# Moving v, the second layer norm and two steps of the max pass to other groups of the loop

## The chip, the cores and the metric

The kernel runs on one core of a Trainium2 chip. The metric is the device time of one execution in microseconds (us). The inputs are 16 sequences of 512 tokens with 128 features, in float32.

## The reference

Per sequence, one transformer layer, with the layer norm behind each residual sum:

```python
qkv = x @ c_attn_w + c_attn_b                      # 128 -> 3 * 128, 16 heads of 8
scores = q k^T / sqrt(8), causal;  attn = softmax(scores)
# heads 0, 1, 2: attn * mult (1.6 in a third of the keys), then normalised again
x = layernorm(x + (attn @ v) @ c_proj_w + c_proj_b)
h = [x, -x];  h = s0 * (h @ W0);  h = relu(h) * 2   # 256 -> 512, weights +-1
h = s1 * (h @ W1);  h = relu(h) * 2                 # 512 -> 512
x = layernorm(x + s2 * (h @ W2))                    # 512 -> 128
```

## The kernel before

**Iterations, groups, steps.** The program is a software pipeline written out by hand. An iteration `n` has four groups of ten steps, and (g, t) below is step t of group g, counted from 0; the words "first group" to "fourth group" are g = 0 to 3. In each step TensorE (PE) does one or two steps of the max pass (`max_scores`, line 946), one step of the scores (`scores`, line 970), in every second step a quarter of the sums of attention times v (`sums`, line 1005), and then what `PLACES` puts there. Work of four sequences runs at once: iteration n does the scores, exponentials and sums of sequence n, the max pass of n and n + 1, q and k of n + 2, v of n + 1, the projection and first layer norm of n - 1 and most of the feed-forward layers of n - 1 and n - 2.

**The max pass.** Before a score is exponentiated the row's maximum is known: PE computes the scores once for `max_ps`, a ring of three PSUM banks, and VectorE (DVE) takes the maximum of each row (`take_max`, line 774). There are 40 such steps in an iteration. `MAX_TWICE` lists the steps with two, `MAX_NONE` those with none; before, the four groups have 13, 10, 7 and 10. The first ten belong to sequence n's last quarter. After the tenth, POOL (GpSimd) splits the maxima into three bf16 parts (`split_rowmax`, lines 529 to 535), PE transposes them ("rowmax1", line 1015, step (1, 0)), DVE copies them out (`take_rowmaxT`, line 796) and ScalarE (ACT) issues a DMA that puts them beside q in `stack` (`rowmax_rows`, line 662). The scores of step (2, 0) wait for that DMA (`rowmax_in[1]`). The same happens with "rowmax0" in (3, 3) and (3, 4) for the next sequence's first half; the scores of (0, 0) of the next iteration wait for it (`rowmax_in[0]`).

**PSUM banks of the fillers.** All work of `PLACES` shares the two banks of `bank_ps` in turn. A row of the table is (what, which sequence, PE's step, the step in which DVE or ACT empties the bank). PE's `claim` waits until the use before the last one has been emptied. ACT empties the feed-forward outputs with two activations, `h_hi` (line 654) and `full` (line 633), behind the exponential of that step.

**v.** Eight fp32 matmul passes on PE (line 1069) and four instructions of DVE (`take_v`, lines 807, 812, 814) in steps (0, 7) and (0, 8), for sequence n + 1. The sums of the next iteration are the first to need it.

**Second layer norm.** `layernorm_stats` and `layernorm_var` (DVE, lines 833, 839, 842, 843), then `normalise_tokens` (POOL, lines 539, 542, 549) and `store` (the DMA to the output, issued by SP). Before, DVE does it for sequence n - 2 in (2, 1) and (2, 2), POOL between two masks of the third group, and SP issues the store as the last item of its iteration. The first layer norm is in (1, 8) and (1, 9), and the transposes of its result, "x1T", in (2, 5).

**SP's queue.** In an iteration SP issues, in this order: nine DMAs that copy the second half of q and k into `stack` (`later_half`, line 379), the load of x for `x_in`, nine DMAs of the first half (`earlier_half`, after the scores of the second group), the load of `x_res` (after it has waited for `rowmax_in[0]`), and the store.

**POOL's queue.** The masks of the exponentials (line 511), the splits of q and k (lines 494, 496), of the maxima, and the low parts of the feed-forward activations (line 519) run on POOL in a fixed order. "ffn1_1", "ffn1_2" and "ffn1_3" have their low parts at the start of the iteration.

Of the kernel before, what the change touches and what calls it, by code (L numbers as in the profile page):

```python
# [49 lines left out]
    ("q", 2, (0, 3), (0, 4)),  # L50
    ("k", 2, (0, 4), (0, 5)),
    ("ffn2T", -2, (0, 5), (0, 7)),
    ("v", 1, (0, 7), (0, 8)),
    ("ffn2", -2, (0, 9), (0, 9)),
    ("rowmax1", 0, (1, 0), (1, 1)),
    ("tok_0", -1, (1, 1), (1, 1)),
# [6 lines left out]
    ("ffn0_2", -1, (3, 0), (3, 1)),  # L63
    ("ffn0_3", -1, (3, 1), (3, 3)),
    ("rowmax0", 1, (3, 3), (3, 4)),
    ("ffn1_0", -1, (3, 6), (3, 7)),
    ("ffn1_1", -1, (3, 8), (3, 9)),
)
# [27 lines left out]

NEGMAX_ROWS = ((3, 5), (1, 2))

LN_STATS = ((1, 8), (2, 1))
LN_VAR = ((1, 9), (2, 2))  # L100
LN_STATS_OF_END = ((1, 2), (3, 4))
LN_VAR_OF_END = ((1, 2), (3, 5))

MAX_TWICE = ((0, 1), (0, 3), (0, 5))
MAX_NONE = ((2, 1), (2, 2), (2, 7))

COPIES_OF_POOL = ((1, 0), (1, 1), (0, 2), (2, 0), (2, 1), (2, 2))
POOL_COPIES_FOR = ((0, 0), (0, 1))
# [27 lines left out]
def block_kernel(nc, x, w_qkv, b_qkv, w_proj, b_proj, k0, k1, k2, s0, s1, s2, out):  # L136
    B, S, D = x.shape
# [17 lines left out]
    def live(b):  # L155
        return 0 <= b.c < B

    def behind_attention(n):

        return n.c == B  # L160
# [15 lines left out]
    def use_of(b, what):  # L176

        return use(b + -BATCH_OF[what], what)

    with ExitStack() as ctx:  # L180
        def sb(name, shape, dt=F32):
            return ctx.enter_context(nc.sbuf_tensor(name, shape, dt))
# [58 lines left out]
        res2 = sb("res2", [P, T, D])  # L241
# [68 lines left out]
        def max_steps(n, g, t):  # L310

            each = [2 if (g_, t_) in MAX_TWICE else 0 if (g_, t_) in MAX_NONE else 1
                    for g_ in range(G) for t_ in range(STEPS)]
# [11 lines left out]
        def last_batch(b):  # L325

            return b.c == B - 1

        def res1_of(b):

            return x_in if last_batch(b) else res1

        def split_by_dve(b, what):

            return last_batch(b) or (behind_attention(b + 2) and what == "ffn1_3")
# [10 lines left out]
        def _(sp):  # L346
# [35 lines left out]
            def store(b):  # L382
                sp.wait_ge(ln_step[1], b.times(4, 4))
                sp.dma_start(out_tok[b.times(1)], res2[:]).then_inc(stored, 16)

            def later_half(n):
                b = n + 1
                if not live(b) or (b.c == 0):
                    return
                sp.wait_ge(split_step, b.times(3, 3))  # L390
                if b.c == 1:
                    sp.wait_ge(stacked[b.parity][0], 9 * 16)
                if live(n + -1):
                    sp.wait_ge(scored, (n + -1).times(G * STEPS, 4 * STEPS))
                stack_half(b, 1)
# [21 lines left out]
                stack_half(b, 0)  # L417

            def iteration(n):
                later_half(n)  # L420
                b = n + 3
                if live(b):
                    wait_full(sp, use_of(b + -1, "xT"))
                    sp.dma_start(x_in[:], x_tok[b.times(1)]).then_inc(x_loaded, 16)
                earlier_half(n)
                if live(n + 1):
                    sp.wait_ge(rowmax_in[0], (n + 1).times(16, 16))
                if live(n):
                    if n.c > 0:
                        wait_free(sp, use_of(n + -1, "proj"))  # L430
                    sp.dma_start(x_res[:], x_tok[n.times(1)]).then_inc(xres_loaded, 16)
                if live(n + -2):
                    store(n + -2)

            run(iteration)
            sp.wait_ge(stored, 16 * B)
# [3 lines left out]
        def _(pool):  # L440
# [112 lines left out]
            def iteration(n):  # L553
                def low(layer, m):
                    b = n + (-2 if layer and m else -1)
                    if live(b) and not split_by_dve(b, f"ffn{layer}_{m}"):
                        low_part_by_pool(b, layer, m)

                def bias_residual():
                    b = n + -1  # L560
                    if live(b):
                        pool.wait_ge(xres_loaded, b.times(16, 16))
                        nc.gpsimd.tensor_tensor(x_res[:], x_res[:], bp[:].unsqueeze(1).broadcast_to([P, T, D]),
                                                ALU.add).then_inc(xres_biased, 1)

                def split_qk(k):
                    b = n + 2
                    if live(b) and not (b.c == 0):
                        split(b, k)

                def layernorm_out(i):
                    b = n + (-2 if i else -1)
                    if live(b):
                        normalise_tokens(b, i)

                def masks(g, k):
                    if live(n):
                        mask(n, g, k)

                def rowmaxes(half):  # L580
                    b = n + (0 if half else 1)
                    if live(b):
                        split_rowmax(b, half)

                low(1, 1)
                low(1, 2)
                low(1, 3)
                masks(0, 0)
                split_qk(0)
                masks(0, 1)  # L590
                rowmaxes(1)
                masks(0, 2)
                split_qk(2)
                bias_residual()
                masks(1, 0)
                masks(1, 1)
                masks(1, 2)
                layernorm_out(0)
                masks(2, 0)
                layernorm_out(1)  # L600
                masks(2, 1)
                low(0, 0)
                masks(2, 2)
                rowmaxes(0)
                low(0, 1)
                low(0, 2)
                low(0, 3)
                masks(3, 0)
                masks(3, 1)
                low(1, 0)  # L610
                masks(3, 2)
# [110 lines left out]
        def _(dve):  # L722
# [107 lines left out]
            def layernorm_stats(b, i, src):  # L830
                wait_free(dve, use_of(b, "ffn2" if i else "proj"))
                for t in range(T):
                    ins = nc.vector.bn_stats(stats[:, t, :], src[:, t, :])
                ins.then_inc(ln_step[i], 1)
# [22 lines left out]
            def iteration(n):  # L857
                for g in range(G):
                    for t in range(STEPS):
                        for b, quarter, step in max_steps(n, g, t):  # L860
                            take_max(b, quarter, step)
                        for what, d, _, step in places(n):
                            b = n + d
# [23 lines left out]
                        for what in SPLIT_STEPS:  # L887
                            b = n + BATCH_OF[what]
# [5 lines left out]
                            elif split_by_dve(b, what):  # L894
# [2 lines left out]
                                if not last_batch(b):  # L897
                                    dve.wait_ge(split_ready, b.times(9, 8))
                                low_part(b, 1 + FT * layer + m, h_hi[layer][:, m, :], h_lo[layer][:, m, :])
                        ln_stats, ln_var = LN_STATS, LN_VAR  # L900
                        if behind_attention(n):
                            ln_stats, ln_var = LN_STATS_OF_END, LN_VAR_OF_END
                        if (g, t) == ln_stats[0] and live(n + -1):
                            layernorm_stats(n + -1, 0, res1_of(n + -1))
                        if (g, t) == ln_stats[1] and live(n + -2):
                            layernorm_stats(n + -2, 1, res2)
                        if (g, t) == ln_var[0] and live(n + -1):
                            layernorm_var(n + -1, 0)
                        if (g, t) == ln_var[1] and live(n + -2):
                            layernorm_var(n + -2, 1)  # L910

            run(iteration)

# [231 lines left out]
```

## Time and profile before

| | us |
|---|---|
| median of 3 runs | 920.17 (919.77 to 925.36) |
| the profiled execution: its time | 922.26 |
| its span in the profile | 919.5 |
| an iteration in the middle of the run | 51.6 |

The profile gives busy time per engine: PE 835.0 us (91%), DVE 621.4 (68%), ACT 608.3 (66%), POOL 527.3 (57%). PE's matmuls are pipelined and their ends are modelled, so a busy PE is not one that nothing holds up: the short waits of its weight loads (PEld) and the chain of waits tell more. TensorE's granted clock is 1.00 of full speed in the middle of the run and 0.96 on the mean of the span, so the middle iterations can be compared with each other.

### The profile page before, as it was taken

Reading aid. Unit: us, or ns where it says so; the run is one execution under the profiler, and the core shown is the slowest. Engines: PE = TensorE matmul, PEld = TensorE weight load, DVE = VectorE, ACT = ScalarE, POOL = GpSimd, SP = SyncE. Lnnn points to the kernel's source line nnn. Section 1 sums busy time; section 2 is a strip of 40 time slices with the busy share of each in tenths; the row PEclk is TensorE's granted clock in tenths of the full one; section 3 lists DMA queues with packets and bytes.
Section 4 is the critical chain, followed back from the end, with each engine's and each line's share of the span. In section 5 each row is a group of like instructions: output and inputs, shape, how many; then the busy total and the mean of one; then the engine's idle time right before and its main releaser. Section 6 shows DMA issues by size and latency. Waiting matters only on the chain.

```text
span 919.5 us, 17053 instructions
## 1 busy us (share of the span) xinstructions
PE 835.0 (91%) x5696; PEld 427.4 (46%) x5696; DVE 621.4 (68%) x2617; ACT 608.3 (66%) x1091; POOL 527.3 (57%) x763
## 2 busy tenths in 40 slices
PE   4488599999999999999999999999999999999875
PEld 1133244545455554545454554545454554545353
DVE  3487386685958587685858587685869587774124
ACT  3036267686776777676776777677776778586743
POOL 4215146575756657575756657575756658384732
PEclk9669699999999999999999999999999999999988
DMA  5735545545353545545352545545353535300000
GB/s 106 87 46 66 65 57 63 68 48 86 42 81 45 74 50 74 67 49 91 36 83 44 74 51 76 63 49 85 45 81 45 77 39 75 50 14 13 24 1 23
DMA packets 65741, 53.16 MB, mean 58 GB/s; under 512 B 5015, under 2 KB 63351, under 8 KB 65655
## 3 DMA queue, kind: packets, MB, share of 16 engines
q1 hardware_dynamic: 63542, 49.72, 39.7%
q0 software_dynamic: 960, 1.58, 1.4%
q10 hardware_dynamic: 1152, 0.79, 0.6%
q8 instruction: 45, 0.74, 0.4%
q14 instruction: 42, 0.34, 0.2%
HBM read 9.24 MB, written 4.19 MB: 15 GB/s over the span
## 4 chain that ended last, share of the span: by engine, by line
PE 60%; DVE 13%; ACT 7%; POOL 7%; issue 7%; DMA 5%; SPq 1%; POOLq 0%; DVEq 0%; ACTq 0%
PE av_ps L1005 11%; PE max_ps L946 11%; PE bank_ps L1032 9%; PE score_ps L970 8%; PE bank_ps L1033 7%; DVE max_ps L774 7%; PE bank_ps L929 4%; POOL res L549 3%; PE bank_ps L1080 3%; DMA stack<-parts 2%; ACT full L633 2%; ACT e L641 2%; DMA stack<-rowmaxT 2%; PE bank_ps L1047 2%; POOL rstd L539 2%
## 5 line engine op out<-in xcount | busy, mean ns | idle before, releaser
L774 DVE CUSTOM_DVE_ANT_0 max_ps<-max_ps,future 128x512 f32<-128x512 f32 (+3 forms) x1024 | 477.6, 517 | 233.9 <-PE max_ps L946 230.4
L641 ACT ACTIVATE e<-score_ps 128x512 f32<-128x512 f32 x640 | 371.3, 613 | 255.9 <-PE score_ps L970 254.6
L946 PE MATMUL max_ps<-stack 72*128 72x512 bf16 (+3 forms) x1024 | 247.6, 312 | 20.8 <-DMA stack<-parts 12.8
L970 PE MATMUL score_ps<-stack 75*128 75x512 bf16 (+3 forms) x1024 | 244.1, 303 | 17.6 <-DMA stack<-rowmaxT 10.6
L511 POOL TENSOR_SCALAR_AFFINE_SELECT e<-e 128x512 f32<-128x512 f32 x256 | 160.1, 637 | 172.2 <-ACT e L641 172.0
L519 POOL TENSOR_TENSOR h_lo<-full,h_hi 128x512 fp32r<-128x512 f32 x119 | 151.5, 1278 | 84.0 <-ACT full L633 83.9
L1005 PE MATMUL av_ps<-e,vaug 128*25 128x512 f32 (+3 forms) x2048 | 191.3, 447 | 0.0
L946 PEld LDWEIGHTS max_ps<-stack 72*128 72x128 bf16 x1024 | 81.3, 99 | 156.5 <-issue 94.0
L774 DVE DVE_READ_ACCUMULATOR2_ANT rowmax<- 128x1 f32 x1024 | 143.8, 140 | 0.0
L970 PEld LDWEIGHTS score_ps<-stack 75*128 75x128 bf16 x1024 | 91.2, 98 | 91.5 <-ACT e L641 35.0
L1032 PE MATMUL bank_ps<-h_hi,w 128*128 128x512 f32 x256 | 109.6, 428 | 0.4 <-DVE h_lo L854 0.4
L1033 PE MATMUL bank_ps<-h_lo,w 128*128 128x512 f32 x256 | 102.7, 401 | 0.0
L654 ACT ACTIVATE h_hi<-bank_ps,scales 128x512 fp32r<-128x512 f32 x128 | 90.8, 709 | 11.0 <-PE bank_ps L1033 10.8
L633 ACT ACTIVATE full<-bank_ps,scales 128x512 f32<-128x512 f32 x128 | 91.6, 716 | 0.0
L1005 PEld LDWEIGHTS av_ps<-e,vaug 128*25 128x25 f32 x2048 | 37.6, 102 | 69.5 <-issue 63.6
L549 POOL TENSOR_SCALAR res<-res,rstd,shift 128x128 f32<-128x128 f32 x120 | 59.5, 509 | 3.1
L1032 PEld LDWEIGHTS bank_ps<-h_hi,w 128*128 128x128 f32 x256 | 49.1, 192 | 24.8 <-ACT full L633 10.6
L539 POOL TENSOR_TENSOR rstd<-var_eps,minus_half 128x4 f32<-128x4 f32 x32 | 32.6, 1017 | 39.6 <-DVE var_eps L843 39.6
L1033 PEld LDWEIGHTS bank_ps<-h_lo,w 128*128 128x128 f32 x256 | 49.1, 192 | 9.2
L494 POOL TENSOR_TENSOR qk<-qk,parts 128x1024 f32<-128x1024 f32 x15 | 32.1, 2140 | 34.6 <-ACT qk L633 34.5
L1080 PE MATMUL bank_ps<-xT,wqk 128*128 128x512 f32 x64 | 39.1, 703 | 1.9 <-ACT xT L633 1.9
L496 POOL TENSOR_TENSOR parts<-qk,parts 128x1024 bf16<-128x1024 f32 x15 | 32.0, 2134 | 11.6 <-ACT parts L716 11.6
(95 smaller groups left out, 725.8 us busy)
## 6 DMA issues: line engine op xcount, KB each, us to landing
stack<-parts SPq DMA_DIRECT2D x276, 128.0 KB
x_in<-in_L_attn_hidden_states SPq DMA_DIRECT2D x16, 256.0 KB, 15.2
x_res<-in_L_attn_hidden_states SPq DMA_DIRECT2D x16, 256.0 KB, 2.9
out_x<-res SPq DMA_DIRECT2D x16, 256.0 KB, 3.4
stack<-parts POOLq DMA_DIRECT2D x12, 128.0 KB, 12.9
stack<-rowmaxT ACTq DMA_DIRECT2D x32, 24.0 KB
e<-in_L_ffn_k SPq DMA_DIRECT2D x1, 256.0 KB, 3.3
e<-in_L_attn_c_attn_w SPq DMA_DIRECT2D x1, 128.0 KB, 2.9
```

The lines of the kernel that those rows point to most:

```text
L511: last = nc.gpsimd.affine_select(out=ap, in_=ap, compare_op=ALU.is_ge, fill=0.0, base=0, pattern=[[0, 4], [1, P]], channel_multiplier=-1)
L519: nc.gpsimd.tensor_tensor(h_lo[layer][:, m, :], whole, hi.bitcast(F32), ALU.subtract).then_inc(split_ready, 1)
L549: ins = nc.gpsimd.tensor_scalar(x[:, t, :], x[:, t, :], rstd[:, i, t:t + 1], shift[:, i, t:t + 1], ALU.mult, ALU.add)
L633: nc.scalar.activation(out_ap, bank_ps[:, u[0], :], func, **kw).then_inc(bank_free[u[0]], 1)
L641: nc.scalar.activation(e[g % 2][:, t, :], score_ps[:, t % 2, :], ACT.Exp, scale=SCALE).then_inc(exped, 1)
L654: nc.scalar.activation(hi, bank_ps[:, u[0], :], func, **kw)
L774: return nc.vector.tensor_tensor_reduce(out=scored_block, in0=scored_block, in1=future[:, P * (T - 1 - qt):S], scale=1.0, scalar=NEG, op0= ...
L946: return nc.tensor.matmul(out_ap[:, col:col + width], st[0:QK_ROWS, h, 0, P * qt:P * qt + P], st[0:QK_ROWS, h, 1, 0:width], start=True, st ...
L970: return nc.tensor.matmul(out_ap[:, col:col + width], st[0:ALL_ROWS, h, 1, P * kt:P * kt + P], st[0:ALL_ROWS, h, 0, P * kt:S], start=True, ...
L1005: last = nc.tensor.matmul(av_ps[32 * j:32 * j + ODD, P * kt:S], vals, src, start=(order == 0 and not odd), stop=(order == 3 and odd == 1))
L1032: nc.tensor.matmul(bank, w, hi, start=(i == 0), stop=False)
L1033: last = nc.tensor.matmul(bank, w, lo, start=False, stop=(i == len(pairs) - 1))
```

## The change

`v` is dropped from (0, 7) and (0, 8) and put at (3, 4) on PE and (3, 5) on DVE, still for sequence n + 1. The max pass gets two more double steps, (0, 7) and (0, 8), and two more empty ones, (1, 1) and (1, 2), so the groups have 15, 8, 7 and 10. The second layer norm of a sequence is done one iteration later, in (0, 0) (DVE), behind the low part of ffn1_1 (POOL), and its store is now the first item of SP's iteration, ahead of `later_half`; only for the last two sequences it stays in the iteration where it was, in (3, 4) and (3, 5).

```diff
-    ("v", 1, (0, 7), (0, 8)),
...
     ("rowmax0", 1, (3, 3), (3, 4)),
+    ("v", 1, (3, 4), (3, 5)),
     ("ffn1_0", -1, (3, 6), (3, 7)),
...
-LN_STATS = ((1, 8), (2, 1))
-LN_VAR = ((1, 9), (2, 2))
-LN_STATS_OF_END = ((1, 2), (3, 4))
-LN_VAR_OF_END = ((1, 2), (3, 5))
-
-MAX_TWICE = ((0, 1), (0, 3), (0, 5))
-MAX_NONE = ((2, 1), (2, 2), (2, 7))
+LN1_STEPS = ((1, 8), (1, 9))
+LN2_STEPS = ((0, 0), (0, 0))
+LN1_STEPS_OF_END = ((1, 2), (1, 2))
+LN2_STEPS_OF_END = ((3, 4), (3, 5))
+
+MAX_TWICE = ((0, 1), (0, 3), (0, 5), (0, 7), (0, 8))
+MAX_NONE = ((1, 1), (1, 2), (2, 1), (2, 2), (2, 7))
...
+        def second_norms(n):
+
+            if live(n + -3) and n.c - 3 < B - 2:
+                yield n + -3, LN2_STEPS
+            if n.c - 2 >= B - 2:
+                yield n + -2, LN2_STEPS_OF_END
...
             def iteration(n):
+                for b, steps in second_norms(n):
+                    if steps == LN2_STEPS:
+                        store(b)
                 later_half(n)
...
-                if live(n + -2):
-                    store(n + -2)
+                for b, steps in second_norms(n):
+                    if steps == LN2_STEPS_OF_END:
+                        store(b)
...
                 low(1, 1)
+                second_layernorm_out(LN2_STEPS)
                 low(1, 2)
...
-                layernorm_out(0)
+                layernorm_out()
                 masks(2, 0)
-                layernorm_out(1)
+                second_layernorm_out(LN2_STEPS_OF_END)
                 masks(2, 1)
```

## Rows read from the trace of the kernel before

**Rows 1.** Busy time by stretch, the four groups of one iteration (columns: stretch, length, five engines, clock, DMA).

```profile
core 0: us, PE busy (x) PEld busy (x) DVE busy (x) ACT busy (x) POOL busy (x), PEclk, DMA share, GB/s
471.00:488.00 17.00, 16.97 (x109) 9.71 (x108) 9.41 (x39) 11.98 (x23) 8.62 (x11) 1.00 0.63 108
488.00:498.70 10.70, 10.34 (x88) 5.39 (x84) 10.43 (x43) 6.97 (x13) 5.82 (x6) 1.00 0.04 10
498.70:509.30 10.60, 9.70 (x73) 4.11 (x73) 9.63 (x49) 8.42 (x17) 9.27 (x17) 1.00 0.52 61
509.30:522.60 13.30, 13.26 (x93) 7.00 (x91) 8.23 (x34) 10.35 (x20) 9.68 (x14) 1.00 0.47 52
```

**Rows 2.** Chain of waits, end of first group and second (columns: start, share, what).

```profile
484.94 1.09 PE bank_ps L1069 x8
...
487.04 0.62 DVE vaug L807 x2
...
489.14 0.69 DVE max_ps L774
...
490.97 0.66 PE bank_ps L929 x4
...
492.84 0.32 PE max_ps L946 x2
```

**Rows 3.** Timeline, PE's weight loads at step (1, 0) (start, length, instruction, idle before).

```profile
487.76 0.23 PEld L1015 LDWEIGHTS bank_ps<-ident_bf,rowmax_parts 128*24 128x24 bf16 x4 [0.48 <-POOL rowmax_parts L535]
```

**Rows 4.** Chain of waits, third group.

```profile
501.71 1.76 POOL res L549 x4
...
507.93 0.59 ACT full L633
```

**Rows 5.** Timeline, third group: second layer norm on DVE, then x1T.

```profile
500.74 0.87 DVE L833 BATCH_NORM_STATS2 stats<-res 128x6 f32<-128x128 f32 x4
...
502.13 0.20 DVE L843 TENSOR_SCALAR var_eps<-moments 128x4 f32<-128x4 f32 x1
...
503.52 0.66 PE L929 MATMUL bank_ps<-ident,res 128*128 128x128 f32 x4 [0.43 <-POOL res L549]
```

**Rows 6.** Timeline, first group: idle time of DVE and POOL.

```profile
474.39 0.70 DVE L774 CUSTOM_DVE_ANT_0 max_ps<-max_ps,future 128x512 f32<-128x512 f32 x1 [2.22 <-PE max_ps L946]
...
476.44 1.27 POOL L519 TENSOR_TENSOR h_lo<-full,h_hi 128x512 fp32r<-128x512 f32 x1 [3.74 <-ACT full L633]
```

**Rows 7.** Timeline, third group: the second layer norm on POOL.

```profile
504.03 1.01 POOL L539 TENSOR_TENSOR rstd<-var_eps,minus_half 128x4 f32<-128x4 f32 x1
...
505.43 2.21 POOL L549 TENSOR_SCALAR res<-res,rstd,shift 128x128 f32<-128x128 f32 x4
```

**Rows 8.** Timeline, fourth group, steps (3, 3) to (3, 6): PE, ACT, PEld.

```profile
461.81 0.38 PE L970 MATMUL score_ps<-stack 75*128 75x384 bf16 x2
...
462.01 0.80 ACT L633 ACTIVATE full<-bank_ps,scales 128x512 f32<-128x512 f32 x1
...
463.35 0.11 PEld L970 LDWEIGHTS score_ps<-stack 75*128 75x128 bf16 x2 [0.32 <-ACT e L641]
```

**Rows 9.** Timeline, DMA issues of SP and ACT, and the scores of (2, 0).

```profile
470.42 7.54 SPq L379 DMA_DIRECT2D stack<-parts  x9
...
490.95 0.74 ACTq L662 DMA_DIRECT2D stack<-rowmaxT  x1
...
498.43 0.79 PE L970 MATMUL score_ps<-stack 75*128 75x512 bf16 x2
...
514.79 0.72 ACTq L662 DMA_DIRECT2D stack<-rowmaxT  x1
...
520.99 0.37 SPq L431 DMA_DIRECT2D x_res<-in_L_attn_hidden_states  x1
```

**Rows 10.** Busy time by stretch, where the second half's transfers end.

```profile
488.00:490.00 2.00, 2.00 (x18) 0.72 (x15) 2.00 (x7) 2.00 (x4) 1.05 (x2) 1.00 0.12 30
```

**Rows 11.** Chain of waits, end of iteration 0.

```profile
98.33 12.43 DMA stack<-rowmaxT
```

**Rows 12.** Timeline, DVE at the start, before the first sequence's scores.

```profile
35.97 0.70 DVE L774 CUSTOM_DVE_ANT_0 max_ps<-max_ps,future 128x512 f32<-128x512 f32 x1 [1.38 <-PE max_ps L946]
```

More of the change, by code:

```diff
@@ L569, in split_qk, with layernorm_out, second_layernorm_out @@
                         split(b, k)
[L571 to L574, printed above, removed]
+                def layernorm_out():
+                    if live(n + -1):
+                        normalise_tokens(n + -1, 0)
+                def second_layernorm_out(steps_of):
+                    for b, steps in second_norms(n):
+                        if steps == steps_of:
+                            normalise_tokens(b, 1)
                 def masks(g, k):
@@ L899, in iteration @@
                                 low_part(b, 1 + FT * layer + m, h_hi[layer][:, m, :], h_lo[layer][:, m, :])
[L900 to L903, printed above, removed]
+                        first_steps = LN1_STEPS_OF_END if behind_attention(n) else LN1_STEPS
+                        if (g, t) == first_steps[0] and live(n + -1):
                             layernorm_stats(n + -1, 0, res1_of(n + -1))
-                        if (g, t) == ln_stats[1] and live(n + -2):
-                            layernorm_stats(n + -2, 1, res2)
-                        if (g, t) == ln_var[0] and live(n + -1):
+                        if (g, t) == first_steps[1] and live(n + -1):
                             layernorm_var(n + -1, 0)
-                        if (g, t) == ln_var[1] and live(n + -2):
-                            layernorm_var(n + -2, 1)
+                        for b, steps in second_norms(n):
+                            if (g, t) == steps[0]:
+                                layernorm_stats(b, 1, res2)
+                            if (g, t) == steps[1]:
+                                layernorm_var(b, 1)
             run(iteration)
```

## The prediction

> **What bounds the kernel now.** I read the busy time of the four groups of one iteration first, then the chain of waits through the same iteration, then the timeline wherever the chain changes engine. The reader should see that no engine bounds the whole iteration: PE is full in the first and fourth group, while DVE has 10.4 busy of 10.7 us in the second and 9.6 of 10.6 in the third [rows 1]. The chain is finer. From the fourth group to step (0, 7) it is PE's own work without a break, v's passes (1.09 us) included. From 486.3 to 490.97 it is DVE: a max step, v (0.62 for its two large instructions), the add of ffn2, two more max steps, rowmaxT, and only then PE's tok_1 transposes [rows 2]. PE then runs to the projection. In the third group the chain is the first layer norm on POOL, the x1T transposes, which waited 0.43 us for it, and ACT until its second `full` at 507.93 [rows 4, 5]. DVE is busy there but is not what the end hangs on. That decides the value of each edit: work leaving DVE in the second group can pay, work leaving it in the third cannot, and work put on PE in the fourth group costs its whole length.
>
> **v leaves the first group, two max steps enter it.** PE loses 1.09 us [rows 2] and does two max steps more, about 0.22 each (one of two narrow blocks took 0.32 [rows 2]; these are one wide block), so it comes to rowmax1's transposes about 0.65 us sooner. They can't go: their weight load already waited for POOL's parts of the maxima, 0.48 us idle before 487.76 [rows 3]. POOL gets there by q's and k's split and a mask, which the change doesn't touch. Part of that 0.48 is PE still streaming the scores before. The start is between 487.3 and 487.76; I take 487.55, a gain of 0.2. From there to tok_1 was 490.97 - 487.76 = 3.2 us. DVE has had two max steps (0.65 each, [rows 2] less overlap) taken early, in time in which it was idle, and no v, so the wait of tok_1 for rowmaxT (about 0.3) goes, and PE itself has two max steps less, 0.32 each [rows 2]: 3.2 - 0.65 - 0.3 = 2.25. So tok_1 starts near 489.8 to 490.0. Gain: **1.0 us per iteration**, bounds 0.6 (the parts come no earlier and DVE's queue stays) and 1.6 (all of v's 1.09 and all waits go). What follows, tok_1 to the projection and the first layer norm, is serial and just starts 1.0 sooner.
>
> **The second layer norm leaves the third group.** On DVE it is 500.74 to 502.3, 1.5 us [rows 5], beside a chain that is on POOL and ACT [rows 4]. Gain 0, bounded by 0.43, x1T's wait, should PE and the first norm somehow move apart. In (0, 0) DVE does it in the 2.22 us it stood idle, POOL its 504.03 to 507.64, 3.6 us, in 3.74 us of idle time [rows 6, 7], for it can begin when the low part of ffn1_1 ends (476.44 - 3.74 = 472.7) and ends about 476.3. The cover nearly fits exactly; if it failed, low(1, 2) would slip by some tenths, and ffn2T needs that only 4 us later. Cost 0.
>
> **v in the fourth group.** PE pays 1.09 at (3, 4). It also waits: v takes the bank that ffn0_3 had, which ACT frees with the `full` of (3, 3), 462.01 to 462.81, while PE is through with the scores of (3, 4) at about 462.2 [rows 8]. That is a new wait of 0.65 (from 0, if the bank were already free, to 0.8). Behind it PE queues the scores of (3, 5) and all of ffn1_0. Back comes what PE waited for ACT at (3, 6): 0.2 of the 0.32 shown [rows 8]. DVE's part, about 1 us, lies beside ffn1_0's long matmuls, in a group where DVE has 5 us free [rows 1]. Loss: 1.09 + 0.65 - 0.2 = **1.5 us per iteration**, bounds 1.1 and 1.9.
>
> **The store ahead of later_half.** SP now waits for POOL's norm (476.3), issues the store and starts the nine stack DMAs near 476.9, not 470.42 [rows 9]. Their consumer, the max pass of (3, 0), is 30 us away. The neighbour matters: rowmaxT's DMA for (2, 0), issued at 490.95 (then about 490), had idle DMA engines, for the nine transfers were over between 488 and 490, 17.6 to 19.6 us after their issue [rows 9, 10]. Shifted, they end near 495.5. How much does that delay it? The other rowmaxT, issued at 514.79 into such traffic, let x_res go at 520.99, 6.2 us [rows 9]; in iteration 0 one took 12.43 us [rows 11]. Both read as if it landed about 2 us behind the traffic. Here that is 497.5; (2, 0) would need it at 498.43 - 1.0 = 497.4. So the wait is about 0.1, from 0 (6.2 us after issue is 496.2) to 5 (by 12.43); x1T's 0.43 of slack hides its first part. I take 0.15 us, in the 12 iterations that have both, near the row of 6.2, which is the steady state.
> The row of 12.43 us is at odds with a rule of the Trainium skill ("DMA: Bandwidth & Descriptors", Queues, rings and completion order): each DMA engine takes turns between the queues it has work for, packet by packet, so a small transfer should slip in between. By the rule this term would be 0 and the sum 1.8 us less.
>
> **Start and end.** In the first iteration v stood before the first maxima; DVE waited 1.38 us for PE there [rows 12]. That goes, v's own DVE time is only moved: -1.4 us, once (0 to -2.4). In iteration 0 the chain ends on a DMA [rows 11], which hides the 0.5. At the end DVE and POOL wait on a serial chain, so the norm of one more sequence lies beside it: 0.
>
> **Sum.** Fourteen full iterations x (1.5 - 1.0) = +7.0; twelve x 0.15 = +1.8; start -1.4: **+7.4 us** on the profiled execution's 922.26 (span 919.5), so 929.7. That execution is 2.1 us above the median of the runs shown, 920.17; on the median it is 927.6, and I say **928**.
>
> **Rivals.**
> *A, the transfer collides* (slower, 0.18). Same terms, but rowmaxT lands 2 us or more after (2, 0) wants it, in twelve iterations: 7.4 - 1.8 + 24 = +30, 950; with half of that 940. It decides once the nine transfers end later than about 495.5. For it: 12.43 us [rows 11]. Against: 6.2 in the steady state. The chance is for a wait of 0.5 us or more.
> *B, the groups balance as DVE's busy time suggests* (faster, 0.19). The second group gives 1.6, and the bank is free when v comes, so 1.1 is lost: -0.5 x 14 - 1.4 = -8.4, 912; if the third group's 1.5 us on DVE paid too, it would be some -29, 891. For it: 10.43 of 10.70 and 9.63 of 10.60 [rows 1]. Against: the chain of the third group has no DVE, and POOL's parts stand before rowmax1 [rows 3, 4]. All but its edge at 912 is a gain over 1%.
> *C, nothing moves* (0.14). PE's waits in the fourth group are partly taken back by waits that I did not see, and the net is within 3 us: 918 to 923. It is inside "no change".
> *D, the change does not do what it says* (0.02, on either side). The tables are plain, and the queues follow them.
>
> **How the numbers follow.** From no change a measurement of this kernel tells about 1%, 9.2 us: 911 to 929.4. My case at 928 has its own range 921 to 935, for a net of 0 to 1.0 us in each of the 14 iterations; it is close to the limit, so it is divided. Forecast 0.47, A 0.18, B 0.19, C 0.14, D 0.02. Within 1%: 0.27 of the forecast, C's 0.14, B's edge 0.02, half of D: 0.44. Slower: 0.20 of the forecast, A's 0.18, half of D: 0.39. Faster: the rest of B, 0.17. Range 909 to 945: it takes in the near part of B and A's half case and leaves out the far ends of both.
>
> **What would show it.** In the changed profile: (1) tok_1's transposes about 1 us closer to step (0, 7), and rowmax1's weight load now waiting longer for POOL; (2) v's weight loads in the fourth group idle 0.5 us or more behind ACT `full`; (3) x1T still released by POOL; (4) the second norm within DVE's and POOL's idle time of the first group; (5) the nine stack DMAs issued 6 us later in the iteration, and PE's scores of (2, 0) with or without a wait on DMA rowmaxT. An iteration should take 52.1 us instead of 51.6. Wrong would be: no wait at v's claim, a second group more than 1.3 us shorter, a third group that shrinks, or a (2, 0) wait over 0.5 us.

## The result: 7.5% slower, and the profile after

| | before | after |
|---|---|---|
| median | 921.5 us (4 runs, 919.8 to 925.4) | 992.4 us (4 runs, 988.1 to 998.2) |
| ratio, 95% interval | | 1.0754 [1.0712, 1.0797] |
| profiled execution: time, span | 922.3, 919.5 | 990.1, 987.9 |
| mean granted clock | 0.964 | 0.906 |

The change costs 71 us where 7.4 were forecast; the time is outside the predicted range. The first thing to read is the list of waits by what they waited for (columns: engine, line, releaser, us in total, times, longest).

```profile
PEld score_ps L985 <- DMA stack<-rowmaxT: 43.3, 13, 8.3
PE score_ps L985 <- DMA stack<-rowmaxT: 38.3, 13, 8.1
```

Before, the scores waited for this DMA twice, both times at the start (in iteration 0 and ahead of iteration 1). The wait ahead of iteration 1 is still there (8.1 us), and twelve iterations are new: (38.3 - 8.1) / 12 = 2.5 us each on PE, and (43.3 - 8.3) / 12 = 2.9 us each by its weight loads, which wait first. The chain of waits of the changed kernel, third group, shows one of them (start, length, what); it answers to [rows 4]:

```profile
518.78 0.23 PE score_ps L985
519.04 10.17 DMA stack<-rowmaxT
529.26 1.03 PE score_ps L985 x2
530.30 1.85 PE av_ps L1020 x8
...
535.51 0.43 PE score_ps L985 x2
...
545.12 0.43 PE bank_ps L1047
...
547.75 0.24 PE bank_ps L1048
```

The chain has no layer norm and no ACT here; it is the transfer. And then something that the prediction did not have: after the wait every piece takes twice its time (0.43 for what is 0.23 elsewhere), until about 546. Busy time by stretch, cut at the issue of the DMA, its landing and the end of the slow pieces, shows it as the granted clock (third column from the end):

```profile
508.00:519.00 11.00, 10.58 (x77) 5.66 (x76) 8.62 (x35) 8.66 (x15) 7.64 (x11) 1.00 0.64 72
519.00:529.30 10.30, 7.16 (x67) 4.08 (x65) 9.06 (x39) 5.05 (x9) 5.78 (x8) 0.96 0.53 72
529.30:546.00 16.70, 16.70 (x74) 6.64 (x74) 6.52 (x27) 9.84 (x18) 5.70 (x11) 0.51 0.46 60
546.00:560.00 14.00, 13.63 (x100) 7.89 (x99) 8.77 (x36) 8.90 (x17) 7.81 (x12) 1.00 0.08 22
```

0.51 is the lower of TensorE's two levels, 1.2 GHz. Over the stretch 200 to 800 us the mean clock is 1.00 before and 0.91 after (same columns; before first, after second):

```profile
200.00:800.00 600.00, 584.91 (x4141) 305.55 (x4140) 436.38 (x1859) 436.06 (x787) 385.07 (x543) 1.00 0.47 63
```

```profile
200.00:800.00 600.00, 561.35 (x3680) 288.41 (x3675) 400.83 (x1664) 391.99 (x700) 341.39 (x485) 0.91 0.41 55
```

In the trace the middle of the run has ten stretches at the lower level, each right behind such a wait: four of 3.4 us, two of 13.7 and four of 17.1. Iterations with one of 3.4 us last 55.5 us, those with 13.7 us 58.5 and those with 17.1 us about 60.8, against 51.6 before.

Why the transfer is late is in the issues of SP and ACT (timeline of the changed kernel; start, length, instruction), which answer to [rows 9]:

```profile
494.42 0.37 SPq L441 DMA_DIRECT2D x_res<-in_L_attn_hidden_states  x1
504.86 0.39 SPq L391 DMA_DIRECT2D out_x<-res  x1
505.35 6.33 SPq L386 DMA_DIRECT2D stack<-parts  x9
```

```profile
519.04 0.74 ACTq L678 DMA_DIRECT2D stack<-rowmaxT  x1
```

SP stands from 494.8 to 504.86 waiting for POOL's norm before it may store, and the nine DMAs queue behind. So rowmaxT is issued 13.7 us behind the nine, not 20.5 to 21.3. The DMA engines, idle at this point before [rows 10], are busy all the way, to read in slices of 2 us (busy time by stretch, after; the last two figures are the engines' share and GB/s):

```profile
521.00:523.00 2.00, 2.00 (x24) 1.46 (x23) 1.98 (x11) 1.57 (x3) 0.82 (x2) 1.00 0.61 68
...
525.00:527.00 2.00, 1.12 (x7) 0.49 (x5) 2.00 (x8) 1.09 (x2) 1.56 (x3) 1.00 0.56 88
527.00:529.00 2.00, 0.00 (x0) 0.00 (x0) 1.66 (x10) 0.00 (x0) 1.17 (x2) 0.89 0.36 77
```

The traffic is not the nine alone. Behind them SP has issued the load of `x_in`, at 511.71, and its landing is in the list of issues from 504 to 530 us (out<-in, issuer, count, size, us from issue to landing):

```profile
x_in<-in_L_attn_hidden_states SPq DMA_DIRECT2D x1, 256.0 KB, 16.0
```

That is 527.7. The packets of rowmaxT itself are moved between 526.5 and 527.9, so it lands with the end of the nine and of this load. (The next nine are issued at 525.99, so the last slice holds some of theirs too.) Iteration 13 has no load of `x_in` any more, and there rowmaxT, again 13.7 us behind the nine, still takes 7.0 us to its last packet, against 7.9 to 9.1 in the iterations with it: most of the delay is the nine's own. No run left that load out by itself.

### The profile page after: what moved, and what is told of

Its sections match the earlier page's. It is cut to its first block, busy times and chain, and to the rows that moved or that the text cites. A ratio compares the mean times of both kernels' runs of the same rounds, so it can differ in the third digit from the quotient of the medians.

```text
span 987.9 us, 17053 instructions
## 1 busy us (share of the span) xinstructions
PE 880.2 (89%) x5696; PEld 444.0 (45%) x5696; DVE 636.7 (64%) x2617; ACT 612.7 (62%) x1091; POOL 521.1 (53%) x763
## 4 chain that ended last, share of the span: by engine, by line
PE 54%; DMA 15%; ACT 14%; POOL 8%; issue 5%; DVE 4%; SPq 1%; POOLq 0%; ACTq 0%; DVEq 0%
DMA stack<-rowmaxT 13%; PE av_ps L1020 12%; PE score_ps L985 10%; PE max_ps L961 9%; PE bank_ps L1047 8%; PE bank_ps L1048 7%; ACT e L657 5%; PE bank_ps L944 3%; POOL qk L505 3%; ACT h_hi L670 3%; ACT full L649 3%; POOL e L522 2%; DVE max_ps L790 2%; PE bank_ps L1084 2%; PE bank_ps L1095 2%
## 5 line engine op out<-in xcount | busy, mean ns | idle before, releaser
L985 PE MATMUL score_ps<-stack 75*128 75x512 bf16 (+3 forms) x1024 | 260.7, 322 | 42.8 <-DMA stack<-rowmaxT 38.3
L961 PE MATMUL max_ps<-stack 72*128 72x512 bf16 (+3 forms) x1024 | 256.4, 327 | 17.0 <-DMA stack<-parts 10.0
L1020 PE MATMUL av_ps<-e,vaug 128*25 128x512 f32 (+3 forms) x2048 | 207.6, 481 | 0.0
L985 PEld LDWEIGHTS score_ps<-stack 75*128 75x128 bf16 x1024 | 96.0, 104 | 124.5 <-DMA stack<-rowmaxT 43.3
L560 POOL TENSOR_SCALAR res<-res,rstd,shift 128x128 f32<-128x128 f32 x120 | 52.5, 451 | 3.1
L1047 PE MATMUL bank_ps<-x_hi,w 128*128 128x512 f32 x64 | 37.6, 588 | 5.7 <-ACT full L649 3.8
## 6 DMA issues: line engine op xcount, KB each, us to landing
stack<-parts POOLq DMA_DIRECT2D x12, 128.0 KB, 12.5
```

The source lines that it names most:

```text
L961: return nc.tensor.matmul(out_ap[:, col:col + width], st[0:QK_ROWS, h, 0, P * qt:P * qt + P], st[0:QK_ROWS, h, 1, 0:width], start=True, st ...
L985: return nc.tensor.matmul(out_ap[:, col:col + width], st[0:ALL_ROWS, h, 1, P * kt:P * kt + P], st[0:ALL_ROWS, h, 0, P * kt:S], start=True, ...
L1020: last = nc.tensor.matmul(av_ps[32 * j:32 * j + ODD, P * kt:S], vals, src, start=(order == 0 and not odd), stop=(order == 3 and odd == 1))
L1047: nc.tensor.matmul(bank, w, hi, start=(i == 0), stop=False)
```

## The experiments

The theory (T): SP's queue is the cause. The nine transfers start late, rowmaxT lands only with the end of SP's traffic, PE stands still at (2, 0), and the standstill costs a second time through the clock. Rivals: the second norm's work in the first group; the tables of v and the max pass; a loss that grows with any delay of the transfers. All ratios are to runs of the kernel before on the same chip in the same session (its medians 920.9 to 922.8). Where an expectation names a rival N, it is the norm's work as the cause.

### The parts alone

**The second layer norm and its store alone** (the tables of v and max as before).

```diff
+    ("v", 1, (0, 7), (0, 8)),
...
-    ("v", 1, (3, 4), (3, 5)),
...
-MAX_TWICE = ((0, 1), (0, 3), (0, 5), (0, 7), (0, 8))
-MAX_NONE = ((1, 1), (1, 2), (2, 1), (2, 2), (2, 7))
+MAX_TWICE = ((0, 1), (0, 3), (0, 5))
+MAX_NONE = ((2, 1), (2, 2), (2, 7))
```

> The kernel before with one part of the change alone: the second layer norm in (0, 0) and its store ahead of later_half; v and the max steps stay. Theory T (the store holds back the nine stack DMAs, so rowmaxT lands late for the scores of (2, 0), and TensorE's clock falls after the wait): nearly the whole loss, 970 to 990 us, waits on DMA rowmaxT of 30 us or more in all, half-clock stretches in the middle. Rival V (v in the fourth group costs): 920 to 925. Rival M (the changes only hurt together): within 1% of before.

Measured: 940.2, ratio 1.017 [1.0105, 1.0234]. The waits are there in every iteration from 3 on, but shorter (same columns as above):

```profile
PE score_ps L985 <- DMA stack<-rowmaxT: 23.8, 14, 7.3
```

That is (23.8 - 7.3) / 13 = 1.3 us each, twelve from iteration 3 on and one in iteration 0, and the clock over 200 to 800 us is 0.98: only four of the twelve waits are followed by a stretch at half clock. The place is right, the size expected too high. In the whole change PE stands still 1.2 us longer each time. I put that down to v and the max steps, which bring rowmaxT's issue to 13.7 us behind the nine, where here it is 14.4, and PE to (2, 0) sooner; with the longer waits the clock falls nearly every time.

**v and the max steps, norm and store as before.**

```diff
-    ("v", 1, (0, 7), (0, 8)),
...
+    ("v", 1, (3, 4), (3, 5)),
...
-MAX_TWICE = ((0, 1), (0, 3), (0, 5))
-MAX_NONE = ((2, 1), (2, 2), (2, 7))
+MAX_TWICE = ((0, 1), (0, 3), (0, 5), (0, 7), (0, 8))
+MAX_NONE = ((1, 1), (1, 2), (2, 1), (2, 2), (2, 7))
```

> The kernel before with the other two parts: v in (3, 4) and (3, 5), max steps 15, 8, 7, 10; the second layer norm and the store stay. My sum without its transfer term: +7.0 - 1.4, so about 926. Theory T: 920 to 930, no wait on rowmaxT in the middle. Rival V: 960 or more.

Measured: 928.8, ratio 1.0078 [1.0054, 1.0103]. An iteration takes 52.2 us. PE's weight loads (timeline: start, length, instruction, idle before) answer to [rows 3, 8] and show both predicted shifts:

```profile
465.04 0.97 PEld L1069 LDWEIGHTS bank_ps<-wv,xT 128*128 128x128 f32 x8 [0.94 <-ACT full L633]
...
491.45 0.21 PEld L1015 LDWEIGHTS bank_ps<-ident_bf,rowmax_parts 128*24 128x24 bf16 x4 [0.74 <-POOL rowmax_parts L535]
...
493.58 0.58 PEld L929 LDWEIGHTS bank_ps<-ident,avT 128*128 128x128 f32 x4
```

rowmax1 to tok_1 is 2.1 us (3.2 before; 2.25 predicted), and rowmax1 waits longer for POOL. v's claim costs PE 9.3 us in 14 times, 0.66 each:

```profile
PEld bank_ps L1069 <- ACT full L633: 13.2, 14, 0.9
PE bank_ps L1069 <- ACT full L633: 9.3, 14, 0.7
```

**The max steps alone**, with v left at (0, 7), and **v alone**:

> The kernel before with only the two max steps moved. By my walk: PE does 0.44 us more before rowmax1 and v stays, so rowmax1 is hardly later, and two narrow steps less come after it: about -0.5 us in each of 14 iterations, 913 to 918. Rival: the steps only queue behind v on DVE, no gain, 921.

> The kernel before with only v moved to (3, 4) and (3, 5). By my sum: PE pays 1.5 us in the fourth group and gets about 0.8 back behind (0, 7): +0.7 in 14 iterations, -1.4 at the start, 928 to 930. Rival (the groups balance): 912 or less. If v's claim waits as I said, its first weight load idles 0.5 us or more behind ACT full.

Measured: max alone 933.1, 1.0126 [1.0085, 1.0167], slower where faster was expected; v alone 934.4, 1.0139 [1.0089, 1.0188], some 5 us above what was expected. Each alone is slower than the two together by its median (1.0078); the intervals overlap a little. Where in the iteration this comes from is in the start times of PE's sums. Each group has its first sums in step 1, so the time from there to the next group's first sums is the length of a group (us, medians of iterations 4 to 11; "v later and max" comes further down):

| | first | second | third | fourth | iteration |
|---|---|---|---|---|---|
| before | 17.65 | 10.50 | 10.52 | 12.94 | 51.62 |
| v and max | 17.31 | 9.83 | 10.52 | 14.54 | 52.20 |
| v alone | 17.31 | 10.05 | 10.51 | 14.54 | 52.42 |
| max alone | 18.29 | 10.63 | 10.51 | 12.94 | 52.38 |
| v later and max | 17.31 | 9.83 | 10.52 | 13.71 | 51.37 |

v leaving gives 0.8 us. The max steps give another 0.2 when v is out of the first group, and cost 0.8 when it is in, 0.6 of it in the first group. The trace of max alone suggests why: DVE has the two extra steps queued in front of v and of ffn2's add, and the transposes of tok_0, behind that add, wait for it, which they did not before:

```profile
PE bank_ps L929 <- DVE res L877: 5.6, 13, 0.4
```

That this is the whole of it was argued from the trace and not tested.

**v alone, one step later**: the same work on PE, only behind ACT's activation.

```diff
-    ("v", 1, (0, 7), (0, 8)),
...
+    ("v", 1, (3, 5), (3, 6)),
```

> The kernel before with only v moved, now to (3, 5) and (3, 6), one step later than in the change, when ACT has emptied ffn0_3's bank. If the claim's wait of 0.66 us is a loss of its own: some 0.4 to 0.6 us less per iteration than with v in (3, 4), 925 to 929 against 934. If ACT only makes PE wait elsewhere: 932 to 936.

Measured: 923.9, 1.0025 [1.0001, 1.0049]. The weight loads' wait for the claim is 2.9 us in all, 0.2 each, against 13.2 at step (3, 4): 10.3 us less, and 10.5 us are back. PE's own matmuls no longer wait there.

### The late transfers alone

**The kernel before, its second-half DMAs held back.** Nothing is moved; SP waits until four steps of the first group's scores are done. Later, three steps and two.

```diff
+                if live(n) and n.c >= 3:
+                    sp.wait_ge(scored, n.times(G * STEPS, 4))
                 stack_half(b, 1)
```

> The kernel before, nothing moved; only SP holds later_half back, from iteration 3 on, until the scores of step (0, 3) are done, some 6 us. Theory T (the time of the nine transfers alone makes the waits): waits of 1 to 2.5 us at the scores of (2, 0) in each iteration from 3 on, as in the run with the second layer norm alone, and 935 to 945 us. Rival N (the second layer norm's own 1.5 us on DVE or 3.6 us on POOL in the first group cost): no more than 925.

> The kernel before, with SP's second-half DMAs held back until three steps of the first group's scores are done. Held until the second step they started only 0.7 us later, until the fourth 6.7 us later (968.8). Here they should start about 4 us later, 16.4 us ahead of rowmaxT's issue. Theory T (rowmaxT lands where the nine transfers end, 21 to 22.4 us after their issue, and (2, 0) needs it 7.5 us after its own issue, so that a wait needs a distance under about 14.5 us): no wait, 920 to 926, rowmaxT's latency 4 to 5 us. Rival (the loss grows with the delay): 4 of 6.7 us of delay for 48 us, 940 to 950.

> The kernel before, with SP's second-half DMAs held back until two steps of the first group's scores are done instead of four. Theory T (rowmaxT's transfer ends only with the nine transfers, about 22 us after their issue, so that a wait arises only where rowmaxT is issued less than about 15 us behind them): the DMAs start about 3 to 4 us later, rowmaxT is issued 17 us behind them, (2, 0) waits for 0 to 0.3 us, no stretch at half clock in the middle: 920 to 926. Rival (the loss grows in proportion to the delay): half of the 48 us, 940 to 948.

Distances and last packets are those of iterations 3 to 13. The waits, by PE's weight loads, are those of iterations 3 to 14:

| held until | ratio | nine DMAs to rowmaxT, issues | rowmaxT's last packet after its issue | PE waits |
|---|---|---|---|---|
| not | 1 | 20.5 to 21.3 us | 1.8 to 1.9 us | none |
| 2 steps | 0.9982 [0.9962, 1.0003] | 19.8 | 1.8 to 3.8 | none |
| 3 steps | 1.0025 [1.0001, 1.005] | 16.3 | 4.7 to 7.2 | up to 0.8, in 3 iterations |
| 4 steps | 1.0509 [1.0466, 1.0551] | 13.8 | 7.7 to 9.1 | 1.6 to 3.4, in 12 iterations |

Four steps: 968.8, where 935 to 945 was expected from the shorter waits of the run with the norm and store alone; these are 2.3 us each on PE. The delay alone costs 48 us, so the norm's work is not needed for the loss (rival N falls). Its waits (the 9.1 is again the one ahead of iteration 1), and its clock over 480 to 540 us:

```profile
PE score_ps L972 <- DMA stack<-rowmaxT: 36.9, 13, 9.1
```

```profile
480.00:500.00 20.00, 19.95 (x127) 11.48 (x126) 11.99 (x53) 13.92 (x26) 9.74 (x11) 1.00 0.27 48
500.00:520.00 20.00, 17.12 (x134) 9.29 (x137) 17.13 (x75) 11.74 (x22) 12.20 (x17) 0.99 0.58 73
520.00:540.00 20.00, 19.49 (x121) 7.93 (x114) 11.18 (x45) 14.25 (x27) 12.74 (x23) 0.76 0.38 48
```

The two-step version is a weak test: it delayed the DMAs by about 1 us and not the 3 to 4 expected. The three-step version is the sharp one. It delays them by 4 to 5 us, where four steps delay them by about 7, and costs 0.25%, not 30 us: the loss is not in proportion to the delay. In the last two rows distance plus latency is 21 to 24 us: rowmaxT lands with the end of the traffic issued before it, and only what is left of that when PE comes is lost.

**The change with the store on POOL's queue**, so that SP goes straight to the nine:

```diff
             def iteration(n):
-                for b, steps in second_norms(n):
-                    if steps == LN2_STEPS:
-                        store(b)
                 later_half(n)
...
                             normalise_tokens(b, 1)
+                            if steps == LN2_STEPS:
+                                pool.wait_ge(ln_step[1], b.times(4, 4))
+                                nc.gpsimd.dma_start(out_tok[b.times(1)], res2[:]).then_inc(stored_by_pool, 16)
```

> The changed kernel, but POOL issues the store itself behind its norm, on its own DMA queue, so SP goes straight to later_half. Theory T: no waits of 1 us or more on rowmaxT in the middle, the clock stays up, and the time falls to that of the run with v and the max steps, 928, plus up to 1.5 us x 13 if POOL's issue costs and the add of ffn2 waits for a store that is stuck in the traffic: 928 to 948. Rival N: above 960.

Measured: 942.3, 1.0229 [1.0192, 1.0266]; 50 of the 71 us are back. The distance is 20.6 us and more again, rowmaxT's last packet comes 1.8 to 2.4 us after issue, the clock over 200 to 800 us is 1.00. What is left of the second norm's part is a new wait, in the view of the DMA's tile:

```profile
L591 POOL DMA_DIRECT2D out_x<-res x14: 850/850/882, 219.8 to 900.3; - x14
...
  DVE res L897: 15.6, 12
...
DMA to landing us min/median/max: 2.3/12.5/13.1
```

The store is issued into the nine and lands after 12.5 us (median) and not 2.3; ffn2's add reuses its buffer and waits 1.3 us in each of 12 iterations.

**The same with SP**: the changed kernel, `later_half` first and then the store.

```diff
             def iteration(n):
+                later_half(n)
                 for b, steps in second_norms(n):
                     if steps == LN2_STEPS:
                         store(b)
-                later_half(n)
```

> The changed kernel with SP issuing the store behind the nine DMAs of the second half instead of ahead of them, nothing else. Theory T: rowmaxT no longer waits, but the store lies behind the nine in the queue and lands 12 us or more after its issue, so ffn2's add in (0, 9) waits for it as with POOL's store (942.3): 938 to 950, no stretch at half clock in the middle. Rival (order in one queue does not matter, the store's own bytes delay rowmaxT): 970 or more.

Measured: 1011.4, 1.0968 [1.0929, 1.1007], worse than the change. The mechanism was as expected and its size not: in the same queue, issued 6 us behind the nine began, the store takes longer still.

```profile
L391 SPq DMA_DIRECT2D out_x<-res x16: 373/385/493, 218.0 to 1002.1; - x16
...
  DVE res L893: 48.2, 12
...
DMA to landing us min/median/max: 2.3/15.5/16.2
```

DVE's add waits 4.0 us each time, PE 3.3 behind it (list of waits), and the clock falls again (0.93 over 200 to 800 us), between 200 and 800 us right behind each of these waits but the shortest (1.4 us):

```profile
PE bank_ps L944 <- DVE res L893: 39.0, 12, 5.2
```

I expected no stretch at half clock and was wrong.

### The clock by itself

**The change with PE kept busy during the wait**: sixteen matmuls of 512 columns without use, ahead of the scores of (2, 0), from sequence 3 on.

```diff
+                if t == 0 and g == 2 and n.c >= 3:
+                    pe.wait_ge(exped, n.times(G * STEPS, STEPS * g + t - 1))
+                    for _ in range(16):
+                        nc.tensor.matmul(out_ap, st[0:QK_ROWS, HALF, 1, 0:P], st[0:QK_ROWS, HALF, 0, :], start=True, stop=True)
                 if t == 0 and g % 2 == 0:
                     pe.wait_ge(rowmax_in[g // 2], n.times(16, 16))
```

> The changed kernel with 16 matmuls of 512 columns put ahead of the scores of (2, 0), from iteration 3 on; what they write is overwritten by the scores. They take 3.4 us at full clock and stand where PE waited 2.3 to 3.8 us. If the idle time at (2, 0) is what lowers TensorE's clock: hardly any half-clock stretch in the middle, and the waits alone remain, 929 + 13 x 3.3 = 965 to 972. If the clock falls for another reason: 990 or more, half-clock stretches as in the changed kernel.

Measured: 963.7, 1.0455 [1.0423, 1.0487], just below the expected range and 29 us less than the change although PE does more. The transfer is as late as in the change (13.7 us behind the nine, last packet 7.8 to 8.9 us after its issue in iterations 3 to 12); only the clock is different:

```profile
L981 PE MATMUL score_ps<-stack 72*128 72x512 bf16 x208 | 47.2, 380 | 0.9 <-ACT e L657 0.5
```

```profile
200.00:800.00 600.00, 583.42 (x4078) 303.62 (x4075) 425.18 (x1762) 412.12 (x742) 360.31 (x515) 1.00 0.43 59
```

So of the 7.5%, 0.8 is v and max (928.8), some 3.8 the standstill (to 963.7) and some 3.0 the clock (to 992.4). The 35 us of the standstill fit 12 waits of 2.9 us. The sixteen matmuls take 3.6 us a time and PE's scores then hardly wait any more, so they last a little longer than the wait did: if anything the clock's part is larger. The Trainium skill ("TensorE: Matmul & The Clock Gate", HAM oscillation) describes a matmul loop that waits for DMA in every round and each time starts again at half rate, which costs time on top of the wait. The trace agrees: with the same late transfer the clock is 0.91 when PE idles and 1.00 when it is kept busy.

### The second norm's work, and a better kernel

**v at (3, 5) with the max steps**, norm and store as before:

> The kernel before with v at (3, 5) and (3, 6) and with the change's two extra and two empty max steps; the second layer norm and the store are left where they were. Theory T (the claim wait is all that v costs in the fourth group, and the max steps pay only when v is out of the first group): 0.66 us a claim wait x 14 becomes about 0.2 x 14, as with v alone (934.4 at step 4, 923.9 at step 5, so -10.5); v and max together took 928.8, so 917 to 921. An iteration takes 51.3 to 51.6 us. Rival: the max steps lose by themselves (0.8 us an iteration when moved alone), and v at step 5 has no more to give: 926 to 933.

Measured: 918.6, ratio 0.996 [0.9944, 0.9977]: the only complete version that is clearly faster than the kernel before, by 0.4%, 4 us. Its v waits no more than that of v alone, one step later (view of line 1069, waits of its weight loads):

```profile
L1069 PEld LDWEIGHTS bank_ps<-wv,xT x128: 186/192/337, 53.6 to 817.9; 128*128 128x128 f32 x128
...
  ACT full L633: 2.9, 14
```

**v at (3, 5) in the changed kernel**, and **in the one with POOL's store**:

> The changed kernel with v at (3, 5) and (3, 6) only. Theory T: the late transfers stay and the claim wait goes; if the parts add, 992 - 10 = 979 to 985, with the waits for rowmaxT at 2 to 4 us. Rival (the iteration is set by the wait for rowmaxT, and PE comes to (2, 0) that much earlier only to wait longer): 988 to 996.

> The changed kernel with the store issued by POOL (as before: 942.3) and v at (3, 5) and (3, 6). It differs from v later and max only in the second layer norm's place. Theory T: 942.3 - 10 = 930 to 934, that is 10 to 15 us more than v later and max, because the residual buffer is kept until the late store and ffn2's add waits for it. Rival (the second norm's move pays once the queue is clear): under 920.

Measured: 980.5, 1.0633 [1.0603, 1.0663], and 931.4, 1.0105 [1.0076, 1.0135]; 11 to 12 us below their versions with v at (3, 4). The parts add here. Moving norm and store costs 1.4 to 1.5% even with the nine on time (1.0105 against 0.996; 1.0229 against 1.0078). Is it the norm or the store? **Both versions without the middle stores**, ffn2's add waiting for POOL's norm:

```diff
-                                nc.gpsimd.dma_start(out_tok[b.times(1)], res2[:]).then_inc(stored_by_pool, 16)
...
-                                    dve.wait_ge(stored_by_pool, b.times(16))
+                                    dve.wait_ge(ln_step[1], b.times(4))
```

The cut shown is against the version whose stores POOL issues; where the norm stays in the third group, SP's store is left out in the same way.

> The changed kernel with v at (3, 5) and (3, 6), from which the stores of all sequences but the last two are left out (their output is never written); ffn2's add waits for POOL's norm instead of the store. To be read against norm before, no store, from which the same stores are left out. With the store issued by POOL the same kernel took 931.4, and the store landed 12.5 us after its issue while ffn2's add waited for it. Theory T (the second norm's computation in (0, 0) costs nothing, only its store does): 914 to 921, within 4 us of the other. Rival (the norm itself disturbs the first group): 10 us or more above the other.

> Later v and max with the stores of all sequences but the last two left out, the second norm in the third group. The control of norm late, no store. It took 918.6 with its stores, which SP issues behind x_res, where nothing of PE waits for them: 914 to 919.

Measured: norm in (0, 0) 917.9, 0.995 [0.9931, 0.9969]; norm in the third group 918.5, 0.9953 [0.9934, 0.9972]. No difference that these intervals of 0.2% either way could show: the norm's computation costs and gives nothing in either place, and the groups of the table above have the same lengths in both. All that its part of the change costs is the store. Where the store stays at the end of SP's iteration it costs nothing (918.6 with it, 918.5 without).

## Why the prediction was wrong

**The failed step is the term "the store ahead of later_half".** It had 0.15 us x 12. Measured: a standstill of PE of 2.5 us x 12 (2.9 by its weight loads, 35 us in all), and 29 us of clock behind it. The ground was laid right: SP's wait for POOL was seen, the distance to rowmaxT was worked out as 490 - 476.9 = 13.1 us and is 13.7, and PE wants the data 20.5 us after the nine's issue (predicted) against 526.1 - 505.35 = 20.8. Only the landing was off: 20.6 us after that issue by the prediction, 529.2 - 505.35 = 23.9 by the trace. Between these numbers there was 0.1 us of margin, so an error of 3 us in the landing was an error of 3 us in the answer.

The error was in how the rows were joined. I took the traffic's end as 18.6 us after the nine's issue from one iteration, [rows 9, 10], called it the end of the nine and did not see the load of `x_in` in it. That iteration was the earliest of all: its load lands 11.6 us after its own issue, the median of the run is 15.2 (lists of issues, first of 470.4 to 489 us, then of the whole run, the kernel before):

```profile
x_in<-in_L_attn_hidden_states SPq DMA_DIRECT2D x1, 256.0 KB, 11.6
```

```profile
x_in<-in_L_attn_hidden_states SPq DMA_DIRECT2D x16, 256.0 KB, 15.2
```

By its packets the traffic ends 18.5 to 21.6 us after the nine's issue in iterations 3 to 12 of the kernel before. Then I added "about 2 us behind the traffic", and used the steady row of 6.2 us [rows 9] only as a bound counted from rowmaxT's own issue. But a transfer that lands behind others must be counted from the others' issue: the later it comes behind them, the shorter its own time looks. The kernel before had that measurement, in one row of the timeline that the prediction did not read beside rowmaxT's:

```profile
498.17 5.97 SPq L379 DMA_DIRECT2D stack<-parts  x9
```

rowmaxT at 514.79 is 16.6 us behind it, and x_res, which waits for its landing, is issued at 520.99 [rows 9]: 22.8 us from the nine's issue. With that, 476.9 + 22.8 = 499.7 against a need at 497.4: 2.3 us of wait, which is rival A. Rival A's mechanism is what happened; its condition (the traffic ends later than 18.6 us after the nine's issue, "about 495.5") was met by some 3 us (by its packets it ends 21.8 us after, at 527.2, in the iteration shown); its price, 950 by waits of 2 us, was too low for waits of 2.9 and lacked the clock.

**The clock** was in no term, though the change could lower it from the 1.00 that [rows 1] and [rows 10] show. A wait on PE's critical path was priced at its own length. Measured: 71 us, where v and max (7) and the standstill (35) alone would make 42.

**The other steps.**
- First and second group: 3.2 us from rowmax1 to tok_1 shortened to 2.25 predicted, 2.1 measured; a gain of 1.0 us per iteration predicted, 0.34 + 0.67 = 1.0 measured (table of the groups). Right for the two together. But the account let the max steps gain whatever else is done, and with v left in place they cost 0.8 us; the expectation of max alone, -0.5 us, failed on that.
- Fourth group: +1.5 us predicted, +1.6 measured. Right.
- v's claim wait: 0.65 predicted, 0.66 measured on PE. Right.
- Net of v and max: +0.5 us per iteration predicted, +0.6 measured; with the start -1.4, 14 x 0.5 - 1.4 = 5.6 against 7.0 by the medians. Right per iteration; that the totals agree as well is partly luck. In the profile of v and max the first sums come 2.9 us later than before, those of iteration 1 come 1.1 us earlier and those of iteration 2 at the same time, so the start's gain is gone by then, and from the last sequence's first sums to the end 1.7 us come back that the sum did not have.
- Second norm out of the third group at no gain, into (0, 0) at no cost: right, to 1 us (the two kernels without stores). The fit beside the low parts is seen in the timeline of after, answering to [rows 6, 7]:

```profile
499.57 0.87 DVE L849 BATCH_NORM_STATS2 stats<-res 128x6 f32<-128x128 f32 x4
```

```profile
501.70 1.01 POOL L550 TENSOR_TENSOR rstd<-var_eps,minus_half 128x4 f32<-128x4 f32 x1 [0.17 <-DVE var_eps L859]
...
503.10 1.74 POOL L560 TENSOR_SCALAR res<-res,rstd,shift 128x128 f32<-128x128 f32 x4
```

- Rival B (the groups balance) had no part: the third group keeps its 10.5 us in each version of the table, and the best one gains 0.4%.
- The rule of the Trainium skill on taking turns between queues ("DMA: Bandwidth & Descriptors", Queues, rings and completion order), as the prediction read it, would have made the term 0. As a guide to when a small transfer lands it did not hold here: rowmaxT's first packet is moved 1.4 us after its issue and the last after 1.8 us on idle engines, but the first after 7.4 to 8.6 us and the last after 7.9 to 9.1 us behind traffic of another queue begun 13.7 us earlier. What holds its packets back is not in the trace.

## What to carry to other kernels

Where a small transfer lands behind a large one, count its landing from the large one's issue, read from a row in which both are seen, and compare it with the consumer's need: here the loss set in steeply (16.3 us of distance cost 0.25%, 13.8 us cost 5%; the norm and store alone, at 14.4 us, cost 1.7%). Read the row in several iterations: the one read here was the earliest. Price an idle PE with the slower matmuls behind it too: here they cost 29 us on top of 35. And a store that waits for a computation has a bad place on either side of a burst of DMAs: ahead of it it holds the burst up, behind it its own buffer comes free late. It was best left where the queue was empty.

## Hardware behaviour that was not expected

- The length of the stretch at the lower clock is not in proportion to the wait. In the changed kernel 17.1 us come behind waits of PE of 2.9 to 3.4 us, but 3.4 us behind 2.2 to 2.6 and 13.7 behind 2.0 and 2.5; in the kernel before with its DMAs held back for four steps, a wait of 2.97 us is followed by 3.4 us, one of 2.05 us by 17.1. Waits of 1.5 to 2.1 us already brought a stretch in four of the twelve iterations of the run with norm and store alone; the others, 0.4 to 1.5 us, brought none. What decides the length is open. PE is busy all through the long ones (16.70 of 16.70 us above).
- The same 256 KB store lands after 2.3 us on idle engines (the changed kernel, issued ahead of the nine), after 12.5 us from POOL's queue into the nine transfers, and after 15.5 us behind them in SP's queue. Neither its own queue nor its place behind the others made it quick.
- PE's dummy matmuls, 47.2 us of work in all, made the kernel 29 us faster.
